# Moving the residual pieces, the second norm and the context sums to other engines and slots in an eight-batch attention and feed-forward kernel

## What is computed

```python
x = x + xattn(layernorm(x), ctx, ctx, Wt, Wp, Wg, Wz, gn_w, gn_b)
x = x + ffn(layernorm(x), up, down, perm)
# xattn(q, k, v): t = Wt@v; p = Wp@q; g = Wg@k
#   att = sum over a group's 64 channels and all columns of p*g
#   y = Wz(group) @ (att*t); group-normalise y; result y*gn_w + gn_b + v
# ffn(x): columns permuted by perm, per head of 128 columns: gelu(t@up[h]) @ down[h], permuted back
```

## Time and profile before

| | us |
|---|---|
| median of three runs (lowest, highest) | 1601.62 (1594.77, 1602.55) |
| profiled execution, its own time | 1599.09 |
| its span from first to last instruction | 1597.3 |
| PE busy | 1518.1 |
| DVE busy | 1285.8 |
| ACT busy | 974.3 |
| POOL busy | 882.6 |

### The profile page before, as it was taken

How to read it: one execution, slowest core, us unless ns; L and a number is a source line. 1 busy time by engine, 2 the same in 40 slices (tenths; PEclk the granted TensorE clock), 3 DMA queues, 4 the chain that set the end, 5 groups by cost and what they waited for, 6 DMA issues and landing times.

```text
span 1597.3 us, 19296 instructions
## 1 busy us (share of the span) xinstructions
PE 1518.1 (95%) x6592; PEld 1234.2 (77%) x6592; DVE 1285.8 (80%) x1736; ACT 974.3 (61%) x1061; POOL 882.6 (55%) x765
## 2 busy tenths in 40 slices
...
GB/s 324 286 297 344 286 211 318 238 296 209 219 276 186 244 149 247 271 185 264 111 253 246 215 236 120 288 219 226 209 165 273 201 248 170 257 152 267 264 283 185
DMA packets 126864, 376.87 MB, mean 236 GB/s; under 512 B 24624, under 2 KB 32816, under 8 KB 118576
## 3 DMA queue, kind: packets, MB, share of 16 engines
...
## 4 chain that ended last, share of the span: by engine, by line
PE 41%; POOL 23%; DMA 13%; DVE 10%; issue 10%; ACT 2%; SPq 1%; POOLq 0%; ACTq 0%; DVEq 0%
PE PP L848 13%; PE PP L834 12%; PE PP L902 6%; PE PP L887 6%; POOL FB L1254 5%; POOL FB L1251 5%; PE PP L861 4%; POOL out L1259 4%; DMA FB<-in_down 4%; DMA FB<-xg_scratch,perm_sb 3%; POOL FB L1239 3%; POOL WW L1200 2%; DMA xg_scratch<-FB 2%; DVE R L1168 2%; DVE R L1016 2%
## 5 line engine op out<-in xcount | busy, mean ns | idle before, releaser
L887 PE MATMUL PP<-GG,WW 128*128 128x512 f32 x1536 | 395.5, 394 | 34.5 <-DVE GG L1163 24.8
L887 PEld LDWEIGHTS PP<-GG,WW 128*128 128x128 f32 x1536 | 287.2, 189 | 106.6 <-issue 46.2
L848 PE MATMUL PP<-R,WC 128*128 128x512 f32 x1536 | 356.1, 393 | 13.7 <-DVE R L1022 7.1
L834 PE MATMUL PP<-R 128*128 128x512 f32 x1536 | 356.7, 392 | 13.0 <-DVE R L1016 11.9
L848 PEld LDWEIGHTS PP<-R,WC 128*128 128x128 f32 x1536 | 290.7, 190 | 78.0 <-issue 10.0
L834 PEld LDWEIGHTS PP<-R 128*128 128x128 f32 x1536 | 288.9, 189 | 76.1 <-issue 12.9
L902 PE MATMUL PP<-R,WW 128*128 128x512 f32 x1050 | 270.7, 393 | 8.3 <-DVE R L1168 6.4
L980 ACT ACTIVATE PP<-PP 128x1024 f32<-128x1024 f32 x256 | 261.5, 1021 | 0.0
L1168 DVE TENSOR_TENSOR R<-PP,R 128x1024 fp32r<-128x1024 f32 x175 | 213.1, 1218 | 56.1 <-ACT PP L980 55.9
L979 ACT ACTIVATE R<-PP 128x1024 fp32r<-128x1024 f32 x175 | 179.6, 1026 | 109.4 <-PE PP L887 107.9
L902 PEld LDWEIGHTS PP<-R,WW 128*128 128x128 f32 x1050 | 195.4, 189 | 55.1 <-issue 13.6
...
## 6 DMA issues: line engine op xcount, KB each, us to landing
...
```

Source lines behind the costliest of these rows:

```text
L834: t = eng.matmul(s_bank(c1), l[:, part(c1)], r, start=(dt == 0 and j == 0), stop=(dt == ND - 1 and j == 2))
L848: t = eng.matmul(PP[2 + ot // 2][:, ot % 2, :], WC[:, l, ct, part(ot)], u[:, r + ct, :], start=(ct == 0 and j == 0), stop=(ct == NT - 1 an ...
L887: t = eng.matmul(PP[slot["up", f, p]][:, e, :], wt[:, l, part(2 * p + e)], g[:, r, :], start=(j == 0), stop=(j == 2))
```

## The change

- The 8 x1_pieces and the squares of batch i (1 to 6) go from the feed-forward of batch i into the s phase of batch i+1 (s0 - 0.3 to s0 + 6.35), load_x and bn_x of batch i+1 follow them, and sum_sq goes from s0 + 5.4 to s0 + 8.6.
- add_c is done by POOL (16 plain additions a batch, each after the bn_x of its rows), and a new stage row_c on ACT takes the row sums of c with 16 Identity activations of 128x512 with an accumulator, whose output goes to FB[4] and isn't used. sum_c and store_sum use these sums directly.
- The turns of batches 1 to 6 stand at s0 + 13.5, 17.7, 21.9, 26.1 instead of 10.2, 15.0, 19.6, 24.2; turn 0 now stands behind y_lo 0.
- The splits of the heads' weights are rearranged: heads 8 and 9 in the y phase of batch 1, heads 4 to 7 somewhat later in that of batch 2, ten others from slot 20. Wg of batch 0 is loaded into SMM; loads of scores in batch 1 stand earlier.

```diff
-TURN = [(15.9, 19.0, 22.3, 25.5)] + [(10.2, 15.0, 19.6, 24.2)] * 6
+TURN = [(15.9, 19.0, 22.3, 25.5)] + [(13.5, 17.7, 21.9, 26.1)] * 6
+CJ = 4
+YHEADS = {1: (8, 9), 2: (4, 5, 6, 7)}
...
+    for k, h in enumerate((10, 11, 12, 13, 14, 15, 0, 1, 2, 3)):
+        t = 20 + 2.2 * k if k < 8 else 4.5 * k + 1
...
-                put(t + 0.25 * ct + late, add_c, i, q, ct)
+                put(t + 0.25 * ct + late, row_c, i, q, ct)
+                put(y0 - 1.5 + 2.4 * q + 0.5 * ct + late, add_c, i, q, ct)
...
-            t = f0 + 5 + 0.8 * k if first else f0 + 3.25 + 2 * X1_UNIT[1 if i == 1 else 2 if last else 0][k] + 0.01 * k
+            t = f0 + 5 + 0.8 * k if first else f0 + 3.25 + 2 * (k + 2) if last else base[i + 1] - 0.3 + 0.95 * k
...
-        e = f0 + 12 if first else f0 + 22.8 if last else base[i + 1] + 5.4
+        e = f0 + 12 if first else f0 + 22.8 if last else base[i + 1] + 8.6
...
+            elif stage == "row_c":
+                i, q, ct = a
+                act.wait_ge(*at["c", i, q])
...
+                    act.wait_ge(*at["cs", i, q - (ct == 0), (ct - 1) % NT])
+                eng.activation(FB[:, CJ, :], RAW[slot["c", i, q]][:, ct, :], ACT.Identity, scale=1.0,
+                               accum_out=sxc[:, ct, q:q + 1]).then_inc(S["cs"], 1)
...
+            elif stage == "add_c":
+                i, q, ct = a
+                pool.wait_ge(*at["c", i, q])
+                pool.wait_ge(*at["x", i, ct])
+                pool.wait_ge(*at["bn1", i, ct, NQ - 1])
+                eng.tensor_tensor(X[:, ct, cols(q)], X[:, ct, cols(q)], RAW[slot["c", i, q]][:, ct, :],
+                                  ALU.add).then_inc(S["xc"], 1)
```

More of the change, by code:

```diff
@@ L177, in y_lo, with row_c @@
         order.append(("y_lo", i, q))
+    def row_c(i, q, ct):
+        if (q, ct) == (0, 0):
+            free["cs", i] = take(("FB", CJ))
+        t = n.up("cs", i, q, ct)
+        give(t, ("raw", slot["c", i, q]))
+        if (q, ct) == (NQ - 1, NT - 1):
+            give(t, ("FB", CJ))
+        order.append(("row_c", i, q, ct))
     def add_c(i, q, ct):
@@ L251, in load_wg @@
     def load_wg(i):
-        k = slot["wg", i] = slot["c", i, 3] if i == 2 else ring("raw", NRAW)
-        free["wg", i] = take(("raw", k))
-        n.dma("wg", i, sem=f"raw{k}")
+        if i == 0:
+            n.dma("wg", 0, sem="wg0")
+        else:
+            k = slot["wg", i] = slot["c", i, 3] if i < 3 else ring("raw", NRAW)
+            free["wg", i] = take(("raw", k))
+            n.dma("wg", i, sem=f"raw{k}")
         order.append(("load_wg", i))
@@ L271, in v_att @@
         if ot == NT - 1:
-            give(t, ("raw", slot["wg", i]))
+            give(t, *([("raw", slot["wg", i])] if i else [("SM", 0), ("SM", 1)]))
         order.append(("v_att", i, ot))
@@ L389, in raw_w @@
     def raw_w(h):
[L391 to L393 removed]
+        for i in YHEADS:
+            if h in YHEADS[i]:
+                return [("raw", slot["c", i, 1 + YHEADS[i].index(h) // 2])]
+        k = 4 if h in (2, 3) else 2 * (h % 2)
         return [("FB", k), ("FB", k + 1)]
     def load_raw(h):
[L397 removed]
+        sem = f"rh{h}" if h in YHEADS[1] + YHEADS[2] else f"rw{2 if h in (2, 3) else h % 2}"
         free["rw", h] = take(*raw_w(h))
```

83 lines of the change are left out of this document (36 added, 47 removed).

## The result

The changed kernel takes **1639.2 us** (median of 4 runs, 1638.4 to 1641.0) against 1600.1 us for the kernel before (median of 4, 1594.8 to 1602.6). The ratio is 1.0237, 95% interval 1.0207 to 1.0266: it is slower by 39 us, where 11 to 13 were forecast; 1639.2 lies inside the stated range of 1575 to 1642, close to its upper end. The profiled execution has a span of 1637.0 us, 39.7 more than before.

A forecast was written before the change was run, and what follows sets the result against it. PE was taken as the bound, busy 1518.1 of 1597.3 us, so only its waits could change. From 1599.1, -28 - 8 + 9 + 38.5 gave 1610.6; the median was set at 1613 us, range 1575 to 1642.

The forecast's parts named there:

- Term 3: y phases, batches 3 to 7: chained turns and stores, lengthened by POOL, make PE wait for y_ev; 38.5 us lost.
- Term 4: Batches 0 and 1: POOL and DVE get relief, against late gathers from heads 8 and 9; 8 us gained, bounds 0 and 14.
- Term 1: Feed-forward: the x1 pieces leave it, and the stretching with them; 28 us gained, bounds 15 and 38.
- Batch 2: Its y phase: same chain, plus POOL issuing loads of heads 4 to 7; 13.7 us waiting, 9 us net loss.
- The rule weighed: DVE and POOL: a shared SBUF port makes whole instructions block each other; the sum would be term 3's upper bound.
- The chain keeps its slack: Rival, y phases: turns start nearer their slots or stores land sooner, PE loses 0 to 1 us a batch; 1568; chance 0.2.
- Stretching and ACT's queue add to the chain: Rival, y phases: 11 us a batch, batch 2 by 14, only 20 gained ahead; 1645; last two rivals 0.2 together.
- POOL is not late: Rival, y phases: the chain of stores alone counts, 4.4 us a batch; 1591 to 1600; chance 0.15.
- the change doesn't do what it says: Rival, feed-forward: waits stay because POOL causes them; gain there 15, time 1626; last two rivals 0.2 together.

The follow-up runs named there:

- e8: e5 with the chain of turns started earlier, plus one added PE wait at y matmul (3,2) from batch 3: 1600.5 us, 23.2 above the same without that wait.
- e3: The kernel before with only the new, later table of turns for batches 1 to 6: 1674.2 us, ratio 1.0473.
- e2: The changed kernel with the additions and row sums back on DVE, all else kept: 1611.9 us, ratio 1.0081.
- e5: e2 with four up-weight loads from batch 3 on issued later, behind the load of Wp's low half: 1587.4 us, ratio 0.9909.
- e12: The changed kernel with plain additions on DVE, row sums left on ACT, up-weight loads later, chain of turns started earlier: 1577.1 us, ratio 0.9846.

## Why the prediction was right and wrong

**The times of the stages were right.** The second norm's xln2 starts at 715.34, which less 11.9 is 703.4, forecast 703.5. Turn 0 starts at 718.4, forecast 718.7. Store 1 starts 4.5 us behind its turn (forecast 3.5; the prediction's own 13.4 less 9.6 give 3.8), and turn 3 ends at 764.3 (forecast 762.2). That end is partly luck: store 0 landed in 5.2 us and store 1 in 8.4, where the sum had 6.2 for both. PE waits for y_ev in every batch, but in two parts: 3.1 to 4.3 us for y_lo of the last quarter, then 4.4 to 6.9 for y_ev, where one wait of 7 to 9 was forecast. The waits for g_lo are 7.9 us in all (forecast under 10), and the scores lose nothing. The waits of batches 3 to 7, 44.2 us together, are near the 39.5 of the sum.

**The step that failed: a term without the clock.** The prediction priced a wait at its length. PE then runs the next 24 matmuls at the lower clock for part of the time, and the ten rows cost 17.6 us beyond the waits. The row that showed it stood ahead of the forecast: six matmuls in 2.90 us behind a wait of 2.39, where 1.52 is normal. It was read as a wait for g_lo only. Another stands in batch 1 of the kernel before:

```profile
216.46 7.29 PE L848 MATMUL PP<-R,WC 128*128 128x512 f32 x24 [2.96 <-ACT Z L933]
```

With the 4.7 us by which the waits were longer, this makes 22.3 of the 24.7 us missed in this term; the rest is spread. e8 measures the price by itself, 1.4 to 1.6 us behind a wait near 5 us; nine of the ten rows of the changed kernel lie at 1.4 to 2.9 us, the tenth (766.90) at nothing.

**Term 3 had the right parts, but weighed them wrongly.** It said that the chain alone (landing 6.2 us a link) gives 4.4 us a batch and POOL's lateness the other 3.5. e3 shows that the turns alone, with no addition on POOL, give a loss of y as large, and e2 that taking POOL out of it gives back 9.5 us in five batches. In e3 and e2 the landing takes POOL's place: store 2 lands in 8.3 to 10.8 us instead of 6.2, in e2 right behind the up-weight loads. e5 moved these loads away: store 2 then lands in 4.6 to 5.2 us, and the kernel is 24.5 us faster. The prediction had 6.2 for all links, from two stores in their old places. In the changed kernel itself it is store 1 that lands late, 8.4 to 9.3 us; in batch 4 the load of Wg (750.01) and two up-weight loads (751.5) are issued beside it. That POOL's lateness puts it there fits, but no run moved these loads alone.

**Term 4 left out the additions.** 8 us gained were forecast for batches 0 and 1, and 5.7 were lost in the profiled executions. The kernels that share this stretch say which half was right: against 231.8 and 232.5 us (before, e3) the rearranged first slots without additions on POOL take 224.4 in the mean, a gain of some 8 us, and with them 234.8. So the additions cost about 10 us (15.1 between the changed kernel and e2, which lie at the two ends of the scatter). The prediction counted DVE's relief, and of POOL's queue only heads 8 and 9. The rows it missed are a pair of waits of 5 us in batch 1:

```profile
195.40 23.68 PE L860 MATMUL PP<-R,WC 128*128 128x512 f32 x96 [4.97 <-ACT Z L955]
224.04 0.77 PE L873 MATMUL PP<-R 128*128 128x512 f32 x1 [4.96 <-DMA R<-wp_scratch]
```

The second comes about on SP's queue, where the load of Wp's low half stands behind Wg's, which waits for the buffer that POOL's last addition frees at 212.6:

```profile
212.81 0.38 SPq L1346 DMA_DIRECT2D RAW<-in_Wg  x1
213.25 0.60 SPq L1356 DMA_DIRECT2D R<-wp_scratch  x1
```

That this load would gain the whole 5 us if it stood ahead of Wg's was not tried.

**Term 1 was too small**, 28 for 35.8. Of the 2.4 us a batch reserved for POOL's own load 0.8 came. The five stretches' PE was busy for 10.2 us less, since before's clock of 0.98 in the stretch shown came back to 1.00; that part was in the 40 us already. **Batch 2** lost 12.0 us for 9; its wait was 11.6 (forecast 13.7), and the row behind it took 8.29 us instead of 5.7. **The end** differs by -3.5 us. No edit touches it, and in the kernels of this study, which share its code, it takes 241.5 to 247.9 us: scatter. **The row sums on ACT** cost nothing, as forecast (e12).

**The rule weighed.** POOL's additions took 1.46 us in the mean over the changed kernel (median 1.30, longest 3.44) against 1.31 alone. The Trainium skill ("SBUF — State Buffer", "SBUF: two separate sides") lets VectorE and GpSimd take turns at a shared port; the trace agrees that they stretch each other, and the median shows how seldom it happened. By it the sum would have been the upper bound of term 3, 11 us of waiting a batch; the waits were 8.1 to 10.0, and 7.1 to 9.8 in e2, where GpSimd adds nothing, so waits of this size don't need the port.

**The rivals.** "The chain keeps its slack" fell with turn 0 at 718.4. "Stretching and ACT's queue add to the chain", 1645, is nearest in time, but that is luck: ACT's part does not show (e12), and stretching is small. "POOL is not late" fell with store 1, and "the change doesn't do what it says" with feed-forwards of 101.7 us.
